# A two-layer hybrid model: in every fourth bank of the first attention core VectorE adds the table for two heads instead of one, and the second layer's feed-forward weights are placed and loaded after the first layer

## The reference

```python
# layer 0, attention a: 4 batches x 16 heads, 1024 x 1024 causal scores, head width 8
scores = jnp.take(causal_kern, jnp.maximum(doff, 0), axis=-1)        # a table by distance i - j, of each batch and head
scores = scores + qm[..., :, None] + km[..., None, :]
scores = scores + MIX * jnp.einsum('bhic,bhjc->bhij', qc, kc) / math.sqrt(CR)
scores = jnp.where(causal, scores, -1000000000.0)
attn = jax.nn.softmax(scores, axis=-1)
ctx = jnp.einsum('bhij,bhjd->bhid', attn, v)
# layer 0, feed-forward: two of eight experts by a gate, squared ReLU, and a shared expert
# layer 1, feed-forward (twice): h = gelu(einsum('nd,edh->neh', xf, w1) + b1); y = einsum('neh,ehd->ned', h, w2) + b2
```

## Time and profile before

| | |
|---|---|
| time, median of 3 runs | 3463.18 us |
| profiled execution: its own time | 3457.46 us |
| its span (first to last instruction) | 3455.7 us |
| mean granted TensorE clock | 0.933 |
| TensorE matmul busy | 3053.0 us (88%) |
| VectorE busy | 2373.2 us (69%) |
| ScalarE busy | 1862.5 us (54%) |
| GpSimd busy | 945.4 us (27%) |
| first attention core, second pass | 235 to 758 us |
| `f0` | 900 to 1078 us |

### The profile page before, as it was taken

One profiled execution on the slowest core, in us unless ns is written; L12 is line 12 of the kernel. 1 busy time (PEld: TensorE's weight loads), 2 busy tenths in 40 slices (PEclk: granted clock), 3 DMA queues, 4 the chain that ended last, 5 costly groups with the idle time before them and its releaser, 6 DMA issues. The chain is left out here.

```text
span 3455.7 us, 67058 instructions
## 1 busy us (share of the span) xinstructions
PE 3053.0 (88%) x25109; PEld 1677.9 (49%) x25109; DVE 2373.2 (69%) x5084; ACT 1862.5 (54%) x3317; POOL 945.4 (27%) x655
## 2 busy tenths in 40 slices
PE   6778999958599999896799969998999999999899
PEld 3234444423276555573222237764455555555676
DVE  6578888848574554666799942235999999998321
ACT  5336666642264332463599924443666666666444
POOL 1029999971001322000000000001222223232100
PEclk8779999989798999897799969999999999999999
DMA  5212333210330000224322210017434344332000
GB/s 169 71 63 94 106 118 109 91 54 24 104 123 25 1 1 1 99 99 157 106 68 67 62 44 1 1 35 219 112 88 99 98 105 106 97 100 68 12 10 13
DMA packets 215138, 260.69 MB, mean 75 GB/s; under 512 B 45211, under 2 KB 165604, under 8 KB 212497
## 3 DMA queue, kind: packets, MB, share of 16 engines
q1 hardware_dynamic: 214849, 256.83, 25.0%
HBM read 200.72 MB, written 56.55 MB: 74 GB/s over the span
## 5 line engine op out<-in xcount | busy, mean ns | idle before, releaser
L1179 POOL TENSOR_TENSOR l0aa_e<-l0aa_e,l0aa_et 128x1024 f32<-128x1024 f32 (+1 forms) x288 | 512.0, 1816 | 44.6 <-ACT l0aa_e L1322 44.5
L2597 ACT ACTIVATE l1ba_sg<-l1ba_sg,l1ba_mn 128x128 f32<-128x128 f32 (+7 forms) x512 | 394.4, 774 | 185.3 <-DVE l1ba_mn L2649 184.2
L2649 DVE CUSTOM_DVE_ANT_0 l1ba_sg<-l1ba_pS,l1ba_tab 128x128 f32<-128x128 f32 (+7 forms) x512 | 368.0, 743 | 40.9 <-PE l1ba_pS L2538 28.5
L1350 DVE TENSOR_REDUCE l0aa_low<-l0aa_pP 128x8 f32<-128x1024 f32 x288 | 343.2, 1220 | 65.8 <-PE l0aa_pP L1203 61.8
L2659 DVE STREAM_TRANSPOSE l1ba_pT<-l1ba_sg 128x1024 f32<-128x1024 f32 (+3 forms) x344 | 367.1, 1067 | 18.5 <-ACT l1ba_sg L2597 13.5
L319 PEld LDWEIGHTS f_pY<-l_w,f_hT 128*128 128x128 f32 x2048 | 268.8, 192 | 122.9 <-issue 119.5
L2559 PE MATMUL l1ba_pO<-l1ba_pT,l1ba_v 32*64 32x256 f32 x9216 | 320.0, 389 | 7.8 <-ACT l1ba_y L2612 7.8
L3027 ACT ACTIVATE l1aa_e<-l1aa_e 128x1536 f32<-128x1536 f32 x192 | 284.4, 1483 | 33.3 <-DVE l1aa_e L3070 21.0
L282 ACT ACTIVATE f_hT<-f_pH,l_b 128x512 f32<-128x512 f32 x256 | 173.9, 687 | 237.4 <-PE f_pH L311 237.2
L2482 POOL TENSOR_TENSOR l1ba_co<-l1ba_co,l1ba_rb 128x1024 f32<-128x1024 f32 x64 | 151.5, 2367 | 544.3 <-ACT l1ba_co L2605 512.5
L1322 ACT ACTIVATE l0aa_e<-l0aa_pS 128x512 f32<-128x512 f32 x432 | 243.0, 593 | 87.0 <-PE l0aa_pS L1236 48.4
(11 more groups left out here) (407 smaller groups left out, 5103.2 us busy)
## 6 DMA issues: line engine op xcount, KB each, us to landing
f_wB<-l0f_weights SPq DMA_DIRECT2D x16, 2048.0 KB, 7.2
l1ba_rb<-l1b_rdd SPq DMA_DIRECT2D x64, 512.0 KB
l0aa_et<-l0a_table SPq DMA_DIRECT2D x16, 1536.0 KB
l1b_qd<-l1bp_part SPq DMA_DIRECT2D x64, 256.0 KB, 2.4
l1ba_qs<-l1b_qd SPq DMA_DIRECT2D x48, 256.0 KB
l0aa_et<-l0a_table SPq DMA_DIRECT2D x16, 512.0 KB
l1ba_tab<-l1b_table SPq DMA_DIRECT2D x32, 256.0 KB
l1ba_qs<-l1b_qd SPq DMA_DIRECT2D x64, 128.0 KB
```

The source lines that it names most:

```text
L1179: nc.gpsimd.tensor_tensor(es, es, t, ALU.mult).then_inc(multiplied, heads)
L1350: nc.vector.tensor_reduce(low1[:, t, :], pP[TURN[quad, t]][:].rearrange("p (u t) -> p u t", t=P), AX.X, ALU.min).then_inc(p1_low, 1)
L2597: nc.scalar.activation(row, row, ACT.Exp, bias=mn[:, r % 2, i + k:i + k + 1], scale=-1.0, accum_out=den[:, r % 2, i + k:i + k + 1]).then_i ...
L2649: nc.vector.tensor_tensor_reduce(row, scores, bias, 1.0, 3e38, ALU.add, ALU.min, mn[:, r % 2, h:h + 1]).then_inc(m_done, 1)
```

## The change

In banks with g % 4 = 1 (36 of 144) only heads 0 and 1 go through ScalarE and GpSimd (`scaled(g)` is 2); for heads 2 and 3 VectorE adds the logarithmic table, and ScalarE takes the exponential of both in one instruction of 128 x 1024. The counts that engines wait for come from lists in place of multiples of `ADDED`. `et` holds five rows instead of four for each quad: heads 0 to 2 for GpSimd, heads 2 and 3 for VectorE, so the table load has two more rows of head 2. The 6 arrays of the second layer's feed-forward weights are allocated when the first layer's are given up, and their 6 loads move from the head of `f0`'s SyncE queue to that of `attention_columns`, behind `load(1, 1)`.

```diff
-    ADDED = 3
+    def scaled(g):
+        return 2 if g % 4 == 1 else 3
+    SCALED = [0] + list(itertools.accumulate(scaled(g) for g in range(QUADS * NB)))
+    ADDED = [QUAD * g - n for g, n in enumerate(SCALED)]
-        et = sb("et", [P, 2, QUAD, SEQ + P])
+        et = sb("et", [P, 2, QUAD + 1, SEQ + P])
             # load_table
-                    for kind, j, n in ((0, 0, ADDED), (1, ADDED, 1)):
+                    for kind, at_head, j, n in ((0, 0, 0, 3), (1, 3, 2, 2)):
             # GpSimd
-                for j, heads in ((0, 2), (2, 1)):
-                    pool.wait_ge(e_done, g * ADDED + j + heads)
+                for j, heads in ((0, 2), (2, 1))[:scaled(g) - 1]:
+                    pool.wait_ge(e_done, SCALED[g] + j + heads)
             # TensorE, second_pass(n)
-                    if before == ADDED:
-                        pe.wait_ge(added, g + 1)
+                    if before >= scaled(g):
+                        pe.wait_ge(added, ADDED[g] + before - scaled(g) + 1)
                     else:
-                        pe.wait_ge(e_done, g * ADDED + before + 1)
+                        pe.wait_ge(e_done, SCALED[g] + before + 1)
-                for at, w in DIAGONAL.get(s // QUAD, ()) if j != ADDED else ():
+                for at, w in DIAGONAL.get(s // QUAD, ()) if j < scaled(n // QUAD) else ():
             # TensorE, weigh(g)
-                pe.wait_ge(multiplied, (g + 1) * ADDED)
+                pe.wait_ge(multiplied, SCALED[g + 1])
             # ScalarE
-                act.wait_ge(added, g + 1)
-                es = e[:, (g * QUAD + ADDED) % E_SLOTS, :]
+                act.wait_ge(added, ADDED[g + 1])
+                slot = g * QUAD % E_SLOTS
+                es = e[:, slot + scaled(g):slot + QUAD, :]
-                if n % QUAD != ADDED:
+                if n % QUAD < scaled(n // QUAD):
             # VectorE, behind first_lows of the same step
-                if n % QUAD == ADDED:
+                if n % QUAD >= scaled(n // QUAD):
                     add_table(n)
             # attention_columns, SyncE
             load(1, 1)
+            load_l1_ffn(sp, D, C)
             # build
-        C = {name: ... for name, shape in (("l1_w1", [16, P]), ("l1_w2", [16, P]), ("l1_b1", [16]), ("l1_gw", [8]), ("l1_gb", [8]), ("l1_rw", [8]))}
+        C = {}
             def ahead(sp):
                 load_l0_attn_b(sp, D, C, W)
-                load_l1_ffn(sp, D, C)
         l0_ffn(nc, D, x, C, "f1", we)
         layer0.close()
+        C.update((name, ...) for name, shape in (("l1_w1", [16, P]), ... the same six ...))
         l1_attn_a(nc, D, x, C, "l1a")
```

More of the change, by code:

```diff
@@ L8 @@
+import itertools
 import math
@@ L1107, in load_table @@
                 if quad >= 2:
-                    sp.wait_ge(multiplied, (quad - 1) * NB * ADDED)
-                    sp.wait_ge(added, (quad - 1) * NB)
+                    sp.wait_ge(multiplied, SCALED[(quad - 1) * NB])
+                    sp.wait_ge(added, ADDED[(quad - 1) * NB])
                 for at, first, w in ((0, 0, SEQ), (SEQ, SEQ - P, P)):
-                    for kind, j, n in ((0, 0, ADDED), (1, ADDED, 1)):
-                        sp.dma_start(et[:, par, j:j + n, at:at + w],
+                    for kind, at_head, j, n in ((0, 0, 0, 3), (1, 3, 2, 2)):
+                        sp.dma_start(et[:, par, at_head:at_head + n, at:at + w],
                                      bass.AP(table.tensor, (kind * HEADS + quad * QUAD + j) * (SEQ + P) + first,
@@ L1154, in table_of @@
                 eng.wait_ge(et_in[quad % 2], 64 * (quad // 2 + 1))
-            t, at = et[:, quad % 2, s % QUAD, :], TABLE_AT[s // QUAD]
+            t, at = et[:, quad % 2, s % QUAD + 1, :], TABLE_AT[s // QUAD]
             if s // QUAD == 7:
@@ L3179, in build @@
         flip = ctx.enter_context(nc.sbuf_tensor("flip", [P, P], F32))
-        C = {name: ctx.enter_context(nc.sbuf_tensor(name, [P] + shape, F32))
-             for name, shape in (("l1_w1", [16, P]), ("l1_w2", [16, P]), ("l1_b1", [16]), ("l1_gw", [8]), ("l1_gb", [8]),
-                                 ("l1_rw", [8]))}
+        C = {}
         layer0 = ctx.enter_context(ExitStack())
@@ L3224, in build @@
         layer0.close()
+        C.update((name, ctx.enter_context(nc.sbuf_tensor(name, [P] + shape, F32)))
+                 for name, shape in (("l1_w1", [16, P]), ("l1_w2", [16, P]), ("l1_b1", [16]), ("l1_gw", [8]), ("l1_gb", [8]),
+                                     ("l1_rw", [8])))
         l1_attn_a(nc, D, x, C, "l1a")
```

## The result

The changed kernel takes 3517.21 us (median of 4 runs, 3513.95 to 3524.26), the kernel before 3462.75 in the same comparison (4 runs, 3461.88 to 3467.84): ratio 1.0169, 95% interval 1.0142 to 1.0196. It is slower by 54.5 us in the medians. The profiled execution took 3513.95 against 3457.46, so 56.5 more. The forecast was +41.8, 3505 us in a range from 3480 to 3528.

What follows compares the result with a forecast made beforehand. The prediction took the loop of TensorE, VectorE and ScalarE, not the full GpSimd, to bound the first attention core. Its terms, 57 - 6.0 - 2.6 - 6.6 = +41.8 us, gave 3505 us, range 3480 to 3528.

Steps and rivals of the forecast that it cites:

- The bound: First core: GpSimd full but nobody waits; TensorE, VectorE, ScalarE loop keeps 32.0 us; rival that GpSimd bounds: 3416 us, 7%.
- The stop per changed bank: First core, `pS` ring: TensorE waits for an add behind VectorE's minima, 1.72 us a bank, 33 banks, +57 us.
- the stop is absorbed: Rival, first core: the 2.6 us TensorE stands anyway per quad swallows stops; in all +5, 3469 us; 6%.
- L1377 gets stuck in more quads: Rival, first core: GpSimd's phase moves, 5 us each, in five quads +25, 3530 us; 7%.
- the clock: Rival, first core: TensorE's clock falls behind stops of 1.9 us, +33, 3538 us; 8%.
- Quad 0: First core's first quad: GpSimd relieved, the 5.71 us L1377 falls under 1 us; -6.0 us, quad about 35.6.
- The last stretch: Last 14 banks of the first core, without tiles, GpSimd the bound: two changed banks save 2.6 us.
- The 9.62 us L1377 that I had left as it is: Last stretch of the first core: this stop stays as it is, bounds -3 and +3 us.
- The weights in `f0`: Stage `f0`: without the six loads ahead, the first gate weights go out earlier; -6.6 us, bounds -11.4 and 0.
- The choice between -11.4 and -6.6: Stage `f0`: -11.4 if the small write lands as in `f1`, -6.6 if `l0b_bfr` holds it; -6.6 taken.
- No new wait in the second core: Second attention core: the six moved loads fit where SyncE waits 15.2 us for TensorE; 0, at worst +3.
- The sum: Whole kernel: 57 - 6.0 - 2.6 - 6.6 = +41.8 us, median 3505 us; the forecast as it stands 72%.

Runs made afterwards that it cites:

- b_light: Kernel before, with GpSimd leaving out head 2's product in banks with g % 4 = 1 and nothing given to VectorE; 3448.74 us, ratio 0.9976.
- d_warm: Kernel after, with seven zero matmuls on TensorE ahead of the stop in most changed banks; 3505.33 us, ratio 1.0136.
- c_order: Kernel after, with the first of VectorE's two adds put ahead of the minima of its step in changed banks; 3462.39 us, ratio 1.0019.
- g_best: Kernel before, with weight loads moved, `l0b_bfr` late, changed banks only at g = 1, 5 and g >= 130, early add; 3434.33 us, ratio 0.9919.
- f_bfr: Kernel before, with layer 1's six weight loads moved and `l0b_bfr` issued at the end of `f0`'s queue; 3448.64 us, ratio 0.9966.
- the weights alone: Kernel before, with only the six layer 1 weight loads moved behind `load(1, 1)`; 3450.84 us, ratio 0.9976.

## Why the prediction was right, and where it was short

**The bound** was read rightly. GpSimd at 32.00 of 32 with nobody waiting for it was not the bound (`b_light`): with 2.3 us less work per quad the quads stayed at 32.0.

**The stop per changed bank** was right in place, cause and size: 1.72 forecast by subtraction from rows of before, 1.70 measured where the clock doesn't interfere (`d_warm`). That the cause is the add's place behind the minima is shown by `c_order`: 0.63 instead of 1.70 for the same work. The rival that the stop is absorbed is refuted, as is the one that L1377 gets stuck in more quads: in after its longest time is 1.83 us.

**The term that was mis-sized is the clock.** The prediction priced it as all or nothing, +33 at 8%, and left it at nothing, because after a stop of 1.12 us the clock had stayed up and after one of 5 us it had fallen. The new stops of 1.59 to 2.51 us lie between, and they do both: 33 stops, and 12 half-rate stretches, each beginning within 1.5 us of the end of such a stop, before or behind it (44 us together, where before had 17). The price is 19.1 us, 1.6 for each stretch. Neither value that the prediction had was right: it is not nothing, and it is not 1.0 behind each of 33 stops. One case at 1.00 stands in the timeline above: the stop at 356.75 was followed by no fall. Here is another of after, at 388.67, with the busy time around it:

```profile
388.67 0.39 PE L1242 MATMUL l0aa_pS<-l0a_qs,l0a_ks 128*128 128x512 bf16 x1 [1.85 <-DVE l0aa_e L1354]
389.99 0.95 PE L1205 MATMUL l0aa_pP<-l0a_ks,l0a_qs 96*128 96x512 bf16 x3
...
391.80 1.06 PE L1205 MATMUL l0aa_pP<-l0a_ks,l0a_qs 96*128 96x512 bf16 x3
```

```profile
385.00:389.00 4.00, 2.15 (x14) 0.87 (x13) 3.79 (x5) 2.10 (x5) 3.07 (x2) 1.00 0.49 149
389.00:393.00 4.00, 4.00 (x22) 1.81 (x22) 1.44 (x2) 2.14 (x3) 3.06 (x2) 0.64 1.00 352
```

The same stop, of the same 1.85 us, and behind this one three tile matmuls take 0.95 and 1.06 us instead of 0.61. The longest but one, 2.38 us, comes twice as well, and the clock fell at 519.96 and not at 670.77. What separates such cases isn't shown; the length of the stop alone doesn't.

**Quad 0.** L1377 is down to 0.27 us from 5.71, as forecast, but from first add to first add the quad takes 38.7 us and not 35.6: the clock falls there twice (239.9 and 257.0), and for twice as long the second time. With the stops filled (`d_warm`) the quad takes 34.8, which is 6.6 less than before apart from its two stops, against 6.0 forecast. The size is right. The cause is shown only in part: in the five kernels that relieve GpSimd in the first banks (after, `b_light`, `c_order`, `d_warm`, `g_best`) L1377 took 0.27 to 0.86 us, but in `f_bfr` it took 1.08 without any relief. So a part of the 6.0 can be gone from an execution of the kernel before as well.

**The last stretch** gained more than forecast. Quad 14, from first add to first add, is 27.2 us instead of 33.2, and it holds one of the 33 stops. Apart from that stop, and with 0.5 us lost again behind this quad, the last stretch is 7.1 us shorter instead of 2.6. The 9.62 us L1377 that I had left as it is also shrank, to 1.83. This hid a part of the clock's price in the sum, and that is luck.

**The weights in `f0`**: -6.6 forecast, -6.7 in after, -6.3 alone, and `wB` issued within 0.2 us of its forecast time. The choice between -11.4 and -6.6 hung on `l0b_bfr`, and `f_bfr` confirms it: with that load away the stage loses 12.0. No new wait in the second core; it was at its shorter length of 335.5 both in after and with the weights alone.

**The sum**: 61.7 in the core against 48.4. The stops are 33 x 1.70 = 56.1, the clock 19.1, quad 0 -6.6 and the last stretch -7.1, together 61.5. The 13.3 above the forecast are 19.1 of clock less 4.5 in the last stretch, 0.6 in quad 0 and 0.7 in the stops. The core and `f0` together make 61.7 - 6.7 = 55.0 of 56.5. The other 1.5 is the net of unchanged stages of -5 to +4 each, of which the second attention core goes with the clock, as shown above.

## What to carry to other kernels

An engine that is busy for all of a loop is its bound only if somebody waits for it; look up the waits on it before you give its work away. When an instruction goes to another engine, ask which buffer it frees and what stands ahead of it in its new queue: here two orders of the same instructions differed by 54 us in one stage, 35 by the stops themselves and 19 by the clock behind them. And take work from a full engine only where it is waited for: changing the last 14 banks alone made the core 17 us shorter, while each of the 33 changed banks ahead of them cost 1.7 us.

## What the runs showed of the hardware

- Of 33 stops of 1.59 to 2.51 us on TensorE 12 were followed by a stretch at half its clock, 3.4 us long and once 6.8, and stops of 0.7 to 1.4 us by none (`c_order`). Filling 1.67 us of such a stop with zero matmuls kept the clock up and gave back 19.1 us in 14 quads, with nothing else changed in the loop (35.5 and 35.6 us a quad, filled and not, where the clock is 1.00).
- Work that no edit touches comes out at one of two lengths: the second attention core at 334.1 to 335.6 us with 17 to 22 us at half clock, or at 340.0 to 340.2 with 33.
- `l0b_bfr` takes 16.1 us to land, and a small write on the same queue is held until then: 10.2 us from the write's issue to the next issue behind its landing, against 1.5 without that load.
- A VectorE `tensor_tensor` of 0.28 to 0.74 us (L1377) took 5.7 us, several GpSimd instructions long, where GpSimd ran without a gap, and 9.6 in the last stretch. In `f_bfr` the same instruction in quad 0, with the same GpSimd work, took 1.1. That the phase between the two engines decides is an inference: no run sets it. In the five kernels with less GpSimd work in the first banks it took 0.27 to 0.86 in quad 0.
